# A stencil layer behind a mixture of experts: the gated expert outputs of pairs 1 to 3 are added onto x by accumulating DMAs of GpSimd's queue

## The chip, the cores and the metric

The kernel runs on one core of one Trainium2 chip. The metric is the device time of one execution in microseconds (us). The core has five engines with a queue of instructions each: TensorE (PE in the profile, its weight loads PEld), VectorE (DVE), ScalarE (ACT), GpSimd (POOL) and SyncE (SP, which here only issues DMAs). They run at the same time and are held in order by semaphores: an instruction raises one, another waits for its value.

## What is computed

Two layers stand one behind the other. The first (left unchanged here) normalises x, chooses two of eight experts for each token, runs the experts, and adds the two expert outputs, each times its gate, onto x. The second is a stencil layer on a field `f` of 8 images of 256 x 256:

```python
def _forward(x, ...):                      # layer 0, mixture of experts
    ...
    y = jnp.einsum('ned,ne->nd', eout, combine)   # two experts per token, weighted by their gates
    return x + y.reshape(x.shape)

def _L1_cond_ref(f, A_grid, B_grid, dt):   # layer 1, stencil
    Af = A_grid[None] * f[:, None]
    Bf = B_grid[None] * f[:, None]
    gradv_Af = _grad(Af[:, 0], 1) + _grad(Af[:, 1], 2)
    gradvv_Bf = _grad2(Bf[:, 0], 1) + _grad2(Bf[:, 1], 2) + _grad(_grad(Bf[:, 2], 2), 1) + ...
    df = -gradv_Af + gradvv_Bf * 0.5
    f_new = f + df * dt[:, None, None]
    return jnp.maximum(f_new, 0.0)
```

`_grad` and `_grad2` are first and second differences along an axis. The field that enters layer 1 is x + gate1 * y1 + gate2 * y2, where y1 and y2 are the rows that the two experts of a token gave.

## The kernel before, in words

A token is one row of 256 floats. x lies in SBUF for the whole kernel as `x_sb` (128 partitions x 16 tiles x 256); the rows of the experts go to a DRAM tensor `y_rows` (y1 first, then y2) by GpSimd's indirect DMAs (`scatter`, L716), 128 rows or 128 KB each.

The stencil stage starts when the last scatter has landed. It works on four **pairs** (g = 0 to 3) of images; a pair is a tile of 128 x 1024 floats (512 KB). Its buffers come twice, by the parity of g: `Y1`, `Y2` (the loaded expert rows; the profile calls both `t_y`), `F0` (x plus the first gated output) and `FV` (the field; the profile calls F0 and FV `t_f`), `FD` (the field times dt, `t_fd`), `GG` (`t_keep`), `GF` (`t_kept`), and products of them. What each engine does for a pair, in the order of its own queue:

- **SyncE**: loads Y1 and Y2 from `y_rows` (L429 in quarters for pair 0, L435 in 512 KB for the others, two pairs ahead at most), and later stores the result of each pair (L439, L444).
- **ScalarE**: `FD` = dt times the field, two halves (L654), when the field is there; then `keep(g+1)` (L630); then `gated(g+1)`: it multiplies the four tiles of Y1 and then the four of Y2 of the next pair by their gates, in place (L641), and raises `t_gated` after each of the two; then the output of the pair before (`relu_out`, L617; for the last pair L667).
- **VectorE**: `center(g)` = GG times the field (L1279); `products(g)`, eight long and four short instructions (L1285 to L1298); `add_up(g+1)`: F0 = Y1 + x (L1245) and FV = Y2 + F0 (L1248), each behind its `t_gated`; `along_columns(g)` (L1303). For pair 0 the gates are applied and the sums made by VectorE itself (L1255).
- **TensorE**: for each pair 20 matmuls of 128 x 512 plus 4 for the columns, all on L896: first `t_kept`, then `t_b0f`, then `t_u`, and the `t_cols` ones of a pair when `along_columns` is done.
- **GpSimd**: nothing after its last scatter.

The order in each queue is the order in which the program is written. `link(...)` makes VectorE wait for its own last instruction to have been written before it goes on (semaphore `chain`).

Of the kernel before, what the change touches and what calls it, by code (L numbers as in the profile page):

```python
# [7 lines left out]
ALU = mybir.AluOpType  # L8
# [8 lines left out]
NB, T, D = 8, 256, 256  # L17
# [103 lines left out]
def moe_then_stencil(nc, x, ids, dt, exp_w1, exp_b1, exp_w2, exp_b2, a_grid, b_grid, small, consts, out):  # L121
# [4 lines left out]
    with ctx:  # L126
# [3 lines left out]
        def sem(name):  # L130
            return ctx.enter_context(nc.semaphore(name))
# [5 lines left out]
        x_sb = sb("x_sb", [P, NJ, D])  # L137
        cst = sb("cst", [P, C_ALL])
        ident = cst[:, C_IDENT:C_IDENT + P]
        gates = sb("gates", [P, TOPK, NJ])  # L140
# [124 lines left out]
        with ExitStack() as phase:  # L265
            def own(name, shape, dt_=F32):
# [3 lines left out]
            Y1, Y2, F0, FV, FD, GG, GF, PA, PB, CC, U1, U2, PP, PQ, SM, OUT = (  # L270
                [own(f"{n}_{par}", [P, 4 * D])[:, :] for par in range(2)]
                for n in ("t_y1", "t_y2", "t_f0", "t_f", "t_fd", "t_keep", "t_kept", "t_a0f", "t_b2f", "t_d1b2f",
                          "t_u1", "t_b0f", "t_pf", "t_qf", "t_cols", "t_out"))
# [49 lines left out]
        y_first = [[sem(f"y{c}_first{i}") for i in range(2)] for c in range(TOPK)]  # L323
        t_first = sem("t_first")
        t_f, t_u2 = sem("t_f"), sem("t_u2")
        t_u1, t_s, t_gf, t_mm, t_relu = (sem(n) for n in ("t_u1", "t_s", "t_gf", "t_mm", "t_relu"))
        t_keep, t_fd, t_gated = sem("t_keep"), sem("t_fd"), sem("t_gated")
        out_dma = [sem(f"out_dma{i}") for i in range(3)]
        grids_ok = sem("grids_ok")
# [8 lines left out]
        block = ctx.enter_context(nc.Block())  # L338

        NPAIR = NB // 2  # L340
        TURNS = 6
        FIRST, ROUNDS = 4, 3
        assert NS == FIRST + TURNS * ROUNDS + 1
# [24 lines left out]
        def _(sp):  # L368
# [60 lines left out]
                    sp.dma_start(buf[0][:, 2 * D * i:2 * D * i + 2 * D].rearrange("p (j d) -> p j d", j=2),  # L429
                                 y_rows_tok[c, :, 2 * i:2 * i + 2, :]).then_inc(y_first[c][i], 16)  # L430
            for g in range(1, NPAIR):
                if g >= 2:
                    sp.wait_ge(t_f, g - 1)
                for c, buf in enumerate((Y1, Y2)):
                    sp.dma_start(buf[g % 2].rearrange("p (j d) -> p j d", j=4),  # L435
                                 y_rows_tok[c, :, 4 * g:4 * g + 4, :]).then_inc(y_in[c][g % 2], 16)
# [4 lines left out]
            g = NPAIR - 1  # L441
# [11 lines left out]
        def _(act):  # L453
# [191 lines left out]
            for g in range(NPAIR):  # L645
                if g >= 2:
                    act.wait_ge(t_s, g - 1)
                    act.wait_ge(t_u2, g - 1)
                for i in range(2):
                    if g == 0 and i == 0:  # L650
                        act.wait_ge(t_first, 1)
                    else:
                        act.wait_ge(t_f, g + 1)
                    last = act.activation(FD[g % 2][:, 512 * i:512 * i + 512], FV[g % 2][:, 512 * i:512 * i + 512],  # L654
                                          ACT.Copy, scale=dt_b[:, 2 * g + i:2 * g + i + 1])
                last.then_inc(t_fd, 1)
                if g < NPAIR - 1:
                    keep(g + 1)
                    gated(g + 1)
                if g >= 1:  # L660
                    relu_out(g - 1)
# [10 lines left out]
        @block.gpsimd  # L672
        def _(pool):
            pool.memset(half[:, :], -0.5).then_inc(half_set, 1)
            pool.wait_ge(half_set, 1)

            def number(out, pattern):

                pool.iota(out, pattern=pattern, base=0, channel_multiplier=0,
                          allow_small_or_imprecise_dtypes=True).then_inc(iota_ok, 1)  # L680


            for i in range(NB + 3):
                if i < NB:
                    pool.wait_ge(var1_ok, i + 1)
                    pool.tensor_tensor(rs1[:, 2 * i:2 * i + 2], var1[:, 2 * i:2 * i + 2], half[:, 0:2],
                                       ALU.pow).then_inc(rs1_ok, 1)
                if i >= 3:
                    pool.wait_ge(var2_ok, i - 2)
                    pool.tensor_tensor(rs2[:, i - 3, :], var2[:, i - 3, :], half[:, 0:KD],  # L690
                                       ALU.pow).then_inc(rs2_ok, 1)
            number(tile_of[:, :], [[P, TOPK * NJ]])
            number(col_of[:, :, :], [[1, NC], [0, TOPK * NJ]])
            number(row_of[:, :, :], [[1, P], [0, TOPK * NJ]])

            def gather(k, m):
                s, par = at_slot(k, m), k % 2
                pool.wait_ge(src_ok, s + 1)
                if k >= 2:
                    pool.wait_ge(tr_done, s - 1)  # L700
                pool.sem_inc(pool_go, 1)
                for t in range(width(k)):
                    pool.indirect_dma_start(  # L703
                        out=gathered[:, par, t, :], out_offset=None, in_=h_rows,
                        in_offset=bass.IndirectOffsetOnAxis(ap=src_cur[:, par, t:t + 1], axis=0),
                    ).then_inc(rows_in[par], 16)

            def scatter(k, m, halves=False):
                s, par = at_slot(k, m), k % 2
                pool.wait_ge(y_half if halves else y_ok, 1 if halves else s + 1)  # L710
                pool.wait_ge(dst_ok, s + 1)
                pool.sem_inc(pool_go, 1)
                for t in range(width(k)):
                    if halves and t == 1:
                        pool.wait_ge(y_ok, s + 1)
                    pool.indirect_dma_start(  # L716
                        out=y_rows, out_offset=bass.IndirectOffsetOnAxis(ap=dst_cur[:, par, t:t + 1], axis=0),
                        in_=y_sb[:, par, t, :], in_offset=None, bounds_check=TOPK * N - 1, oob_is_err=False,
                    ).then_inc(y_out[par], 16)

            pool.wait_ge(hrows_out, 16 * NJ)
            for k in range(FIRST):
                gather(k, None)
            for k in range(2, FIRST):
                gather(k + 2, None)
                scatter(k - 2, None)
            with pool.Fori(1, ROUNDS + 1) as m:
                for k in range(FIRST, FIRST + TURNS):
                    gather(k + 2, m)
                    scatter(k - 2, m)  # L730
            scatter(NS - 3, None)
            scatter(NS - 2, None)
            scatter(NS - 1, None, halves=True)


        @block.tensor
# [186 lines left out]
        def _(dve):  # L923
            steps = [0]

            def link(ins):

                steps[0] += 1
                ins.then_inc(chain, 1)
                dve.wait_ge(chain, steps[0])  # L930
# [99 lines left out]
            for c, src in enumerate((lg, lg2)):  # L1030
# [4 lines left out]
                                              op0=ALU.mult, op1=ALU.add))  # L1035
# [200 lines left out]
                ends = v.rearrange("p r (s c) -> p r s c", c=4)  # L1236
                return ends[:, :, 0:D // 4:D // 4 - 1, :]

            def add_up(g):
                if g >= 2:  # L1240
                    dve.wait_ge(t_fd, g - 1)
                if g > 0:

                    dve.wait_ge(t_gated, 2 * g - 1)
                    link(dve.tensor_tensor(F0[g % 2], Y1[g % 2],  # L1245
                                           x_sb[:, 4 * g:4 * g + 4, :].rearrange("p j d -> p (j d)"), ALU.add))
                    dve.wait_ge(t_gated, 2 * g)
                    last = dve.tensor_tensor(FV[g % 2], Y2[g % 2], F0[g % 2], ALU.add)  # L1248
                else:
                    for i in range(2):  # L1250
                        for c, y, dst in ((0, Y1, F0), (1, Y2, FV)):
                            dve.wait_ge(y_first[c][i], 16)
                            for j in range(2 * i, 2 * i + 2):
                                at = slice(D * j, D * j + D)
                                last = dve.scalar_tensor_tensor(  # L1255
                                    out=dst[0][:, at], in0=y[0][:, at], scalar=gates[:, c, j:j + 1],
                                    in1=x_sb[:, j, :] if c == 0 else F0[0][:, at], op0=ALU.mult, op1=ALU.add)
                            if c == 0:
                                link(last)
                        if i == 0:  # L1260
                            last.then_inc(t_first, 1)
                last.then_inc(t_f, 1)

            def wide(v):
# [7 lines left out]

            def center(g):
                par = g % 2
                dve.wait_ge(t_f, g + 1)
                dve.wait_ge(t_keep, g + 1)
                if g >= 2:
                    dve.wait_ge(t_mm, g - 1)
                dve.tensor_tensor(GF[par], GG[par], FV[par], ALU.mult).then_inc(t_gf, 1)  # L1279

            def products(g):
                par = g % 2
# [20 lines left out]
                dve.tensor_tensor(rows_of(SM[par])[:, :, 1:D - 1], pv[:, :, 2:D], qv[:, :, 0:D - 2],  # L1303
                                  ALU.add).then_inc(t_s, 1)

            add_up(0)
            for g in range(NPAIR):
                center(g)
                products(g)
                if g + 1 < NPAIR:  # L1310
                    add_up(g + 1)
                along_columns(g)


# [19 lines left out]
```

## Time and profile before

| | us |
|---|---|
| Time before, median of 3 runs | 395.35 (393.88 to 395.98) |
| The profiled execution: its own time | 395.92 |
| its span in the trace | 393.8 |
| VectorE busy | 284.7 (72% of the span) |
| ScalarE busy | 256.3 (65%) |
| TensorE matmuls busy | 330.6 (84%) |
| GpSimd busy | 130.0 (33%) |
| Stencil stage, from the first center to the end | 337.24 to 393.8 |

The profile's page has busy times of the engines, the span in 40 equal slices of 9.85 us (a digit is the busy share in tenths), DMA queues, the chain of work that ended last, and groups of instructions by line. The trace behind it can be asked for the instructions in order of time, for waits, for the chain piece by piece, for DMAs, and for the busy time within given stretches. A line number is that of the kernel before. The median of the runs and the profiled execution's time differ by 0.57 us; the span is 2.12 us shorter than the profiled execution's time.

### The profile page before, as it was taken

The numbers are of one execution on the slowest core, as the hardware profiler recorded it, in microseconds if no ns is written. First come the engines' busy times: TensorE is split into PE (matmuls) and PEld (weight loads), VectorE is DVE, ScalarE is ACT, GpSimd is POOL, SyncE is SP. The second block draws the span as 40 slices with busy tenths as digits, with TensorE's granted clock in tenths as the row PEclk, the third lists the DMA queues.
The fourth block names the chain that finished last, engine by engine and source line by source line (L and its number), as shares of the span: only waits on it lengthen the run. The fifth ranks groups of instructions, "written<-read, shape, count | busy, mean of one in ns | idle before, by whom it ended". The sixth has DMA issues, their size and how long they took to land.

```text
span 393.8 us, 7288 instructions
## 1 busy us (share of the span) xinstructions
PE 330.6 (84%) x2424; PEld 298.4 (76%) x2424; DVE 284.7 (72%) x500; ACT 256.3 (65%) x467; POOL 130.0 (33%) x103
## 2 busy tenths in 40 slices
PE   1676232889999999999999999999999991687976
PEld 1565232889999999999999999999999990233422
DVE  4696773657767768678777776866876852999994
ACT  2578032677696988779779779887976822543521
POOL 1245304233415545543551543554454031000000
PEclk9998655789999999999999999999999997599999
DMA  8903252973657776865775776677577004631111
GB/s 278 322 27 106 83 214 65 318 245 101 229 194 248 263 256 216 287 186 197 267 250 153 258 248 238 241 262 242 188 230 253 0 31 113 208 106 53 53 54 53
DMA packets 49204, 72.21 MB, mean 183 GB/s; under 512 B 3229, under 2 KB 40479, under 8 KB 49056
## 3 DMA queue, kind: packets, MB, share of 16 engines
q1 hardware_dynamic: 45056, 62.13, 47.1%
q0 software_dynamic: 3792, 9.45, 7.5%
q10 hardware_dynamic: 336, 0.39, 0.3%
q8 instruction: 10, 0.16, 0.2%
q14 instruction: 10, 0.08, 0.1%
HBM read 63.56 MB, written 9.31 MB: 185 GB/s over the span
## 4 chain that ended last, share of the span: by engine, by line
PE 70%; DVE 15%; DMA 5%; issue 4%; ACT 3%; POOL 2%; SPq 0%; POOLq 0%; DVEq 0%; ACTq 0%
PE psum L847 32%; PE psum L869 29%; PE psum L896 3%; PE psum L826 2%; DMA raw_b<-in_L_cond_exp_w_dram 2%; PE psum L813 1%; DMA t_y<-y_rows 1%; DVE st L965 1%; DMA x_sb<-in_x_dram 1%; POOL rs L690 1%; DVE t_f L1245 1%; DVE t_b0f L1290 1%; DVE t_pf L1297 1%; DVE t_cols L1303 1%; DVE t_kept L1279 1%
## 5 line engine op out<-in xcount | busy, mean ns | idle before, releaser
L847 PE MATMUL psum<-slot_h,w_split 128*128 128x256 f32 (+1 forms) x1104 | 136.4, 284 | 4.3 <-DVE slot_h L1147 4.3
L847 PEld LDWEIGHTS psum<-slot_h,w_split 128*128 128x128 f32 x1104 | 134.6, 196 | 4.9 <-issue 4.9
L869 PE MATMUL psum<-w_split,hid 128*128 128x256 f32 x936 | 117.8, 285 | 0.2 <-issue 0.2
L869 PEld LDWEIGHTS psum<-w_split,hid 128*128 128x128 f32 x936 | 113.7, 192 | 0.3 <-issue 0.3
L703 POOL DMA_INDIRECT gathered<-h_rows,src_cur x40 | 60.3, 1507 | 143.7 <-DVE src_cur L1130 109.3
L564 ACT ACTIVATE relu<-psum,b_cur 128x256 f32<-128x256 f32 (+1 forms) x184 | 70.0, 444 | 19.9 <-PE psum L847 15.1
L1141 DVE TENSOR_TENSOR w_split<-raw_b,w_split 128x2048 fp32r<-128x2048 f32 x23 | 52.7, 2292 | 22.1 <-ACT w_split L546 22.1
L1135 DVE TENSOR_TENSOR w_split<-raw_a,w_split 128x2048 fp32r<-128x2048 f32 x23 | 52.6, 2287 | 18.7 <-ACT w_split L539 11.4
L1154 DVE TENSOR_TENSOR hid<-relu,hid 128x512 fp32r<-128x512 f32 (+1 forms) x92 | 52.8, 605 | 17.6 <-ACT hid L573 16.2
L716 POOL DMA_INDIRECT y_rows<-y_sb,dst_cur x39 | 52.4, 1344 | 29.3 <-DVE y_sb L1173 13.2
L539 ACT ACTIVATE w_split<-raw_a 128x2048 fp32r<-128x2048 f32 x23 | 44.2, 1921 | 26.9 <-DMA raw_a<-in_L_cond_exp_w_dram 26.7
L573 ACT ACTIVATE hid<-relu 128x512 fp32r<-128x512 f32 (+1 forms) x92 | 50.5, 581 | 0.0
L546 ACT ACTIVATE w_split<-raw_b 128x2048 fp32r<-128x2048 f32 x23 | 44.4, 1932 | 4.0 <-DMA raw_b<-in_L_cond_exp_w_dram 4.0
L654 ACT ACTIVATE t_fd<-t_f,dt_b 128x512 f32<-128x512 f32 x8 | 5.5, 717 | 28.6 <-DVE t_f L1248 20.1
L1147 DVE TENSOR_TENSOR slot_h<-psum,slot_h 128x512 fp32r<-128x512 f32 (+1 forms) x23 | 14.0, 609 | 12.3 <-ACT slot_h L553 10.4
L896 PE MATMUL psum<-t_kept,cst 128*128 128x512 f32 x16 | 9.4, 719 | 12.5 <-DVE t_kept L1279 12.5
L826 PE MATMUL psum<-cst,gathered 128*128 128x128 f32 x80 | 13.3, 282 | 5.7 <-DMA gathered<-h_rows,src_cur 5.7
L778 PE MATMUL psum<-eye_rw,hT 128*128 128x136 f32 x64 | 12.6, 360 | 6.3 <-ACT hT L494 6.2
L778 PEld LDWEIGHTS psum<-eye_rw,hT 128*128 128x128 f32 x64 | 11.0, 254 | 8.1 <-ACT hT L494 6.2
L1173 DVE TENSOR_TENSOR y_sb<-psum,b_all 128x512 f32<-128x512 f32 (+1 forms) x23 | 13.6, 593 | 4.0 <-PE psum L869 4.0
L553 ACT ACTIVATE slot_h<-psum 128x512 fp32r<-128x512 f32 (+1 forms) x23 | 12.6, 546 | 6.0 <-PE psum L826 6.0
L896 PEld LDWEIGHTS psum<-t_kept,cst 128*128 128x128 f32 x16 | 3.5, 223 | 16.6 <-DVE t_kept L1279 12.7
(157 smaller groups left out, 282.8 us busy)
## 6 DMA issues: line engine op xcount, KB each, us to landing
raw_a<-in_L_cond_exp_w_dram SPq DMA_DIRECT2D x23, 1024.0 KB, 7.9
raw_b<-in_L_cond_exp_w_dram SPq DMA_DIRECT2D x23, 1024.0 KB
t_y<-y_rows SPq DMA_DIRECT2D x6, 512.0 KB, 4.9
x_sb<-in_x_dram SPq DMA_DIRECT2D x4, 512.0 KB, 7.1
h_rows<-h_tok SPq DMA_DIRECT2D x16, 128.0 KB, 2.2
out_dram<-t_out SPq DMA_DIRECT2D x3, 512.0 KB, 2.9
b_all<-in_L_cond_exp_b_dram SPq DMA_DIRECT2D x1, 1024.0 KB, 9.8
t_y<-y_rows SPq DMA_DIRECT2D x4, 256.0 KB, 3.7
```

Source lines behind the costliest of these rows:

```text
L539: act.activation(w_split[:, 0, par, 0, :], w1_raw[par], ACT.Copy).then_inc(w1_hi, 1)
L546: act.activation(w_split[:, 1, par, 0, :], w2_raw[par], ACT.Copy).then_inc(w2_hi, 1)
L564: last = act.activation(relu[:, bank, i, 0:n], banks[bank][:, ST * i:ST * i + n], ACT.Relu, bias=b1_cur[:, par, blk:blk + 1])
L573: act.activation(hid[:, par, 0, 2 * bank:2 * bank + 2, 0:n], relu[:, bank, :, 0:n], ACT.Copy).then_inc(hid_hi, 1)
L703: pool.indirect_dma_start(out=gathered[:, par, t, :], out_offset=None, in_=h_rows, in_offset=bass.IndirectOffsetOnAxis(ap=src_cur[:, par, ...
L716: pool.indirect_dma_start(out=y_rows, out_offset=bass.IndirectOffsetOnAxis(ap=dst_cur[:, par, t:t + 1], axis=0), in_=y_sb[:, par, t, :], i ...
L847: last = pe.matmul(banks[bank][:, ST * (blk % 2):ST * (blk % 2) + rows], w_split[:, 0, par, w, at:at + P], slot_h[:, par, h, k, 0:rows], s ...
L869: last = pe.matmul(banks[bank][:, D * t:D * t + D], hid[:, par, h, blk, P * t:P * t + P], w_split[:, 1, par, w, D * blk:D * blk + D], star ...
L896: return pe.matmul(banks[2 * g + q].rearrange("p (i d) -> p i d", i=2), w, v[:, k, :, :], start=start, stop=stop)
L1135: dve.tensor_tensor(w_split[:, 0, par, 1, :], w1_raw[par], w_split[:, 0, par, 0, :].bitcast(F32), ALU.subtract).then_inc(w1_lo, 1)
L1141: dve.tensor_tensor(w_split[:, 1, par, 1, :], w2_raw[par], w_split[:, 1, par, 0, :].bitcast(F32), ALU.subtract).then_inc(w2_lo, 1)
L1154: dve.tensor_tensor(hid[:, par, 1, 2 * bank:2 * bank + 2, 0:n], relu[:, bank, :, 0:n], hid[:, par, 0, 2 * bank:2 * bank + 2, 0:n].bitcast( ...
```

## The change

Pairs 1 to 3 no longer have `add_up`. When ScalarE has gated Y1 of a pair, GpSimd issues a DMA that reads Y1 from SBUF and adds it to the pair's 128 x 1024 floats of `x_sb`, in place; when that has landed and Y2 is gated too, a second DMA adds Y2. Its semaphore `y2_added` is what ScalarE's FD, VectorE's center and SyncE's load of pair 3 now wait for; the field of pairs 1 to 3 is read from `x_sb` (`field(g)`) and no longer from FV. Pair 0 is as it was.

```diff
+        def field(g):
+            return FV[0] if g == 0 else x_sb[:, 4 * g:4 * g + 4, :].rearrange("p j d -> p (j d)")
...
             for g in range(1, NPAIR):
-                if g >= 2:
-                    sp.wait_ge(t_f, g - 1)
+                if g == 2:
+                    sp.wait_ge(t_f, 1)
+                elif g > 2:
+                    sp.wait_ge(y2_added, 16 * (g - 2))
                 for c, buf in enumerate((Y1, Y2)):
...
                     if g == 0 and i == 0:
                         act.wait_ge(t_first, 1)
+                    elif g == 0:
+                        act.wait_ge(t_f, 1)
                     else:
-                        act.wait_ge(t_f, g + 1)
-                    last = act.activation(FD[g % 2][:, 512 * i:512 * i + 512], FV[g % 2][:, 512 * i:512 * i + 512],
+                        act.wait_ge(y2_added, 16 * g)
+                    last = act.activation(FD[g % 2][:, 512 * i:512 * i + 512], field(g)[:, 512 * i:512 * i + 512],
...
             scatter(NS - 1, None, halves=True)
+
+            for g in range(1, NPAIR):
+                pool.wait_ge(t_gated, 2 * g - 1)
+                pool.dma_start(field(g), Y1[g % 2], accum_op=ALU.add).then_inc(y1_added, 16)
+                pool.wait_ge(t_gated, 2 * g)
+                pool.wait_ge(y1_added, 16 * g)
+                pool.dma_start(field(g), Y2[g % 2], accum_op=ALU.add).then_inc(y2_added, 16)
...
-            def add_up(g):
-                if g >= 2:
-                    dve.wait_ge(t_fd, g - 1)
-                if g > 0:
-
-                    dve.wait_ge(t_gated, 2 * g - 1)
-                    link(dve.tensor_tensor(F0[g % 2], Y1[g % 2],
-                                           x_sb[:, 4 * g:4 * g + 4, :].rearrange("p j d -> p (j d)"), ALU.add))
-                    dve.wait_ge(t_gated, 2 * g)
-                    last = dve.tensor_tensor(FV[g % 2], Y2[g % 2], F0[g % 2], ALU.add)
-                else:
...
             def center(g):
                 par = g % 2
-                dve.wait_ge(t_f, g + 1)
+                if g == 0:
+                    dve.wait_ge(t_f, 1)
+                else:
+                    dve.wait_ge(y2_added, 16 * g)
                 dve.wait_ge(t_keep, g + 1)
                 if g >= 2:
                     dve.wait_ge(t_mm, g - 1)
-                dve.tensor_tensor(GF[par], GG[par], FV[par], ALU.mult).then_inc(t_gf, 1)
+                dve.tensor_tensor(GF[par], GG[par], field(g), ALU.mult).then_inc(t_gf, 1)
...
-            add_up(0)
+            add_up()
             for g in range(NPAIR):
                 center(g)
                 products(g)
-                if g + 1 < NPAIR:
-                    add_up(g + 1)
                 along_columns(g)
```

VectorE's queue from the last products of pair 0 to the first of pair 1, before (the names in brackets are the semaphores that an instruction waits for):

```order
L1298 TENSOR_TENSOR t_qf<-gr,t_fd 128x1024
L1245 TENSOR_TENSOR t_f_1<-t_y_1,x_sb 128x1024 [waits t_gated,chain]
L1248 TENSOR_TENSOR t_f<-t_y_1,t_f_1 128x1024 [waits t_gated,chain]
L1303 TENSOR_TENSOR t_cols<-t_pf,t_qf 128x4x254
L1279 TENSOR_TENSOR t_kept<-t_keep,t_f 128x1024 [waits t_keep,t_f]
L1285 TENSOR_TENSOR t_b2f<-gr,t_fd 128x1024 [waits t_fd]
```

The same place now:

```order
L1306 TENSOR_TENSOR t_pf<-gr,t_fd 128x1024
L1307 TENSOR_TENSOR t_qf<-gr,t_fd 128x1024
L1312 TENSOR_TENSOR t_cols<-t_pf,t_qf 128x4x254 [waits chain]
L1288 TENSOR_TENSOR t_kept<-t_keep,x_sb 128x1024 [waits t_keep,y2_added]
L1294 TENSOR_TENSOR t_b2f<-gr,t_fd 128x1024 [waits t_fd]
```

The two additions are gone from between the products and the columns, the columns now wait for the products directly, and center waits for the semaphore of the second accumulating DMA.

GpSimd's queue at its end, now (in the kernel before it ended with the last scatter into y_rows):

```order
L725 DMA y_rows<-y_sb,dst_cur 4096x256 [waits y_ok]
L746 DMA x_sb<-t_y_1 128x1024 [waits t_gated]
L749 DMA x_sb<-t_y_1 128x1024 [waits y1_added,t_gated]
L746 DMA x_sb<-t_y_0 128x1024 [waits t_gated]
L749 DMA x_sb<-t_y_0 128x1024 [waits y1_added,t_gated]
```

Two DMAs for each pair were added, the second of each behind the landing of the first; pair 3 has the same two rows again.

ScalarE's queue from the gating of pair 1 to that of pair 2, now (before, the row of L663 read t_f and waited for t_f, at L654, with the same rows around it):

```order
L648 ACTIVATE t_y_1<-t_y_1,gates 128x256 [waits y1_in1]
L648 ACTIVATE t_y_1<-t_y_1,gates 128x256 x3
L663 ACTIVATE t_fd<-x_sb,dt_b 128x512 [waits y2_added] x2
L637 ACTIVATE t_keep<-grid,ones,dt_n 128x512 [waits t_gf]
L637 ACTIVATE t_keep<-grid,ones,dt_n 128x512
L648 ACTIVATE t_y_0<-t_y_0,gates 128x256 [waits y0_in0]
```

Nothing moved in ScalarE's queue; the gating of the next pair stands behind the instruction that waits for the second accumulating DMA of this pair.

## Rows read from the trace of the kernel before

**Rows 1.** Busy time by stretch: busy us (instructions) of each engine, granted clock, DMA.

```profile
core 0: us, PE busy (x) PEld busy (x) DVE busy (x) ACT busy (x) POOL busy (x), PEclk, DMA share, GB/s
325.00:337.24 12.24, 1.00 (x9) 0.79 (x7) 3.95 (x9) 2.24 (x3) 1.54 (x2) 0.68 0.52 157
337.24:350.60 13.36, 11.12 (x20) 4.60 (x20) 13.22 (x15) 6.33 (x13) 0.00 (x0) 0.78 0.28 93
350.60:363.96 13.36, 11.10 (x24) 4.31 (x24) 13.22 (x16) 6.77 (x14) 0.00 (x0) 1.00 0.36 118
363.96:377.32 13.36, 11.10 (x24) 4.31 (x24) 13.22 (x17) 6.85 (x14) 0.00 (x0) 1.00 0.11 39
```

**Rows 2.** The chain of work that ended last, around pair 1's additions and the end.

```profile
345.91 1.15 DVE t_qf L1298
...
347.08 1.24 DVE t_f L1245
348.31 0.02 issue
348.33 0.04 DVE t_f L1248
348.37 1.11 issue
349.48 1.21 DVE t_cols L1303
...
384.90 5.52 PE psum L896 x12
```

**Rows 3.** Timeline, VectorE and ScalarE from pair 1's gating: start, us, engine, line.

```profile
339.28 3.29 ACT L641 ACTIVATE t_y<-t_y,gates 128x256 f32<-128x256 f32 x8
...
348.33 1.23 DVE L1248 TENSOR_TENSOR t_f<-t_y,t_f 128x1024 f32<-128x1024 f32 x1
...
349.60 1.33 ACT L654 ACTIVATE t_fd<-t_f,dt_b 128x512 f32<-128x512 f32 x2 [7.02 <-DVE t_f L1248]
...
352.25 3.29 ACT L641 ACTIVATE t_y<-t_y,gates 128x256 f32<-128x256 f32 x8
...
356.47 24.43 SPq L439 DMA_DIRECT2D out_dram<-t_out  x3
```

**Rows 4.** Timeline, the start of pair 3 on ScalarE and VectorE.

```profile
376.39 1.34 ACT L654 ACTIVATE t_fd<-t_f,dt_b 128x512 f32<-128x512 f32 x2 [6.51 <-DVE t_f L1248]
377.32 1.22 DVE L1279 TENSOR_TENSOR t_kept<-t_keep,t_f 128x1024 f32<-128x1024 f32 x1
...
378.45 1.22 DVE L1285 TENSOR_TENSOR t_b2f<-gr,t_fd 128x1024 f32<-128x1024 f32 x1
```

**Rows 5.** The instructions on the gated rows of pairs 1 to 3, min/median/max ns.

```profile
L641 ACT ACTIVATE t_y<-t_y,gates x24: 491/493/496, 339.3 to 368.5; 128x256 f32<-128x256 f32 x24
```

**Rows 6.** Timeline, the last scatter and the first load behind it.

```profile
326.03 0.42 DVE L1173 TENSOR_TENSOR y_sb<-psum,b_all 128x256 f32<-128x256 f32 x1 [2.34 <-PE psum L869]
...
327.23 0.98 POOL L716 DMA_INDIRECT y_rows<-y_sb,dst_cur  x1 [1.68 <-DVE y_sb L1173]
329.36 1.91 SPq L429 DMA_DIRECT2D t_y<-y_rows  x4
```

**Rows 7.** DMA issues by line: count, KB each, median us to landing.

```profile
t_y<-y_rows SPq DMA_DIRECT2D x6, 512.0 KB, 4.9
...
out_dram<-t_out SPq DMA_DIRECT2D x3, 512.0 KB, 2.9
...
out_dram<-t_out SPq DMA_DIRECT2D x2, 256.0 KB, 2.2
```

**Rows 8.** Timelines of VectorE and of GpSimd at two long indirect DMAs.

```profile
289.93 2.29 DVE L1135 TENSOR_TENSOR w_split<-raw_a,w_split 128x2048 fp32r<-128x2048 f32 x1 [1.01 <-ACT w_split L539]
...
301.04 2.29 DVE L1135 TENSOR_TENSOR w_split<-raw_a,w_split 128x2048 fp32r<-128x2048 f32 x1 [1.17 <-ACT w_split L539]
...
290.36 2.69 POOL L703 DMA_INDIRECT gathered<-h_rows,src_cur  x1 [0.31 <-issue]
...
302.22 1.98 POOL L716 DMA_INDIRECT y_rows<-y_sb,dst_cur  x1 [0.30 <-issue]
```

**Rows 9.** Timeline, TensorE's first matmuls of the stencil stage.

```profile
338.52 3.78 PE L896 MATMUL psum<-t_kept,cst 128*128 128x512 f32 x4 [12.53 <-DVE t_kept L1279]
...
377.45 1.98 PE L896 MATMUL psum<-t_cols,cst 128*128 128x512 f32 x4 [2.21 <-DVE t_cols L1303]
```

More of the change, by code:

```diff
@@ L326, in moe_then_stencil @@
         t_u1, t_s, t_gf, t_mm, t_relu = (sem(n) for n in ("t_u1", "t_s", "t_gf", "t_mm", "t_relu"))
+        y1_added, y2_added = sem("y1_added"), sem("y2_added")
         t_keep, t_fd, t_gated = sem("t_keep"), sem("t_fd"), sem("t_gated")
@@ L1237, in edge_cols, with add_up @@
                 return ends[:, :, 0:D // 4:D // 4 - 1, :]
-            def add_up(g):
-                if g >= 2:
-                    dve.wait_ge(t_fd, g - 1)
-                if g > 0:
-                    dve.wait_ge(t_gated, 2 * g - 1)
-                    link(dve.tensor_tensor(F0[g % 2], Y1[g % 2],
-                                           x_sb[:, 4 * g:4 * g + 4, :].rearrange("p j d -> p (j d)"), ALU.add))
-                    dve.wait_ge(t_gated, 2 * g)
-                    last = dve.tensor_tensor(FV[g % 2], Y2[g % 2], F0[g % 2], ALU.add)
-                else:
[L1250 to L1261, printed above, removed]
+            def add_up():
+                for i in range(2):
+                    for c, y, dst in ((0, Y1, F0), (1, Y2, FV)):
+                        dve.wait_ge(y_first[c][i], 16)
+                        for j in range(2 * i, 2 * i + 2):
+                            at = slice(D * j, D * j + D)
+                            last = dve.scalar_tensor_tensor(
+                                out=dst[0][:, at], in0=y[0][:, at], scalar=gates[:, c, j:j + 1],
+                                in1=x_sb[:, j, :] if c == 0 else F0[0][:, at], op0=ALU.mult, op1=ALU.add)
+                        if c == 0:
+                            link(last)
+                    if i == 0:
+                        last.then_inc(t_first, 1)
                 last.then_inc(t_f, 1)
```

## The prediction

> **What bounds the kernel now.** I read the busy time by stretch first, then the chain of work that ended last, then the instructions in order of time. From 337.24 us to the end the kernel is in the stencil stage. The stretches of [rows 1] are one pair each: VectorE is busy 13.22 of every 13.36 us, ScalarE 6.3 to 6.9, TensorE 11.1, GpSimd not at all. The chain of [rows 2] runs through VectorE alone (the "issue" pieces of about 1.1 us are time in which the next VectorE instruction was already running or being written) until the columns of pair 2, and from there through TensorE, twelve matmuls in 5.52 us at the end. So an instruction taken off VectorE in pairs 0 to 2 is worth its time, as long as nothing else comes last. The reader is to see in [rows 3] what stands behind that: ScalarE waits 7.02 us for pair 1's field, because it had gated the pair's rows long before VectorE came to add them (gated from 339.28 on, added at 347.08).
>
> **What is removed.** Two additions for each of three pairs. From the first of them to the columns: 349.48 - 347.08 = 2.40 us [rows 2]. The columns follow the products directly, and their wait for the products costs what the wait between t_qf and L1245 cost, 0.02 to 0.03, which is inside this difference. VectorE's own work per pair falls from 13.36 to 10.96 us, over three pairs by 7.2 us. That is the floor: no gain beyond it.
>
> **What is added, and where it lies.** The sum of a pair now takes two DMAs one behind the other. Call L the time from the release of one of them (the end of the gating, or the landing of the first) to the landing seen by whoever waits. The work between two pairs becomes a loop that VectorE is not in:
>
> - Pair 1: Y1 is gated at 339.28 + 3 x 0.40 + 0.49 = 340.97 (eight activations in 3.29 us, each 0.49 long, so 0.40 apart) [rows 3, 5]. Y2's gating takes another 1.60 us and lies beside the first DMA. So the field of pair 1 is there at 340.97 + 2L.
> - From a field to the next pair's gated Y1 ScalarE does FD, keep and four gatings: before from 349.56 (end of L1248) to 352.25 + 1.69 = 353.94, so 4.38 us [rows 3]. All of this order stays, and is now behind the landing.
> - Field of pair 2: 340.97 + 2L + 4.38 + 2L. Field of pair 3: 340.97 + 8.76 + 6L = 349.73 + 6L.
> - From the last field on, the end is as before: FD takes 1.34 us after a start 0.04 behind the field, and t_b2f needs it, at the field + 1.41. Before, t_b2f of pair 3 started at 378.45 [rows 4]. The end moves by 349.73 + 6L + 1.41 - 378.45 = **6L - 27.3 us**, as long as this is above -7.2.
>
> So six DMAs in a row decide, and the change breaks even at L = 4.55 us. VectorE stays the bound only if 4.38 + 2L is under 10.96, so for L under 3.3.
>
> **What L is.** The trace has no accumulating DMA, and no plain one of GpSimd. The nearest row is GpSimd's last scatter [rows 6]: VectorE's write ends at 326.45, GpSimd starts at 327.23 and is busy for 0.98 us, and the load of SyncE that waited for the landing starts at 329.36. From release to release that is 2.91 us for 128 KB. Four times the bytes: the stores of 512 and 256 KB land in 2.9 and 2.2 us [rows 7], so 0.7 us for each 256 KB, and 384 KB more are 1.05 us. A copy would be 3.96 us. An accumulation has to read the old values of x too; I take these as another 512 KB at the same rate, 1.4 us. **L = 5.4 us.** The lower end: GpSimd starts at once (0.78 less) and the second read is hidden (1.4 less), 3.2; the store of SyncE in 2.9 is nearly the same. The upper end: the loads of 512 KB that shared the engines landed in 4.9, which is 2.0 over the store [rows 7]; added to 5.4, and with 1.2 for a wait on VectorE (below), 8.6. I take the value near the scatter's row, since it is the only one of GpSimd's own queue to start in the same way.
>
> Beside it, the store of the pair before: ScalarE's output of it follows the gatings, and the store was issued at 356.47, 6.9 us after the field [rows 3], when the first accumulation of the next pair (from 4.4 to 9.8 us after the field) moves its bytes. Its 512 KB cost up to 1.4 us there, in pairs 2 and 3; half of it each is 1.4 in all. The loads of pair 3 start at the field of pair 1 and land within 4.9, before the accumulation moves bytes: nothing. Center on VectorE reads `x_sb` in place of FV, the same size: nothing. Behind the wait of ScalarE's FD stand keep, the gatings and the output of the pair before; all but the output are in the 4.38, and the output's store has a pair's time. SyncE's stores stand behind its load of pair 3, which waits for pair 1's field, well before the first store is due. GpSimd has nothing behind its DMAs.
>
> The sum: 6 x 5.4 - 27.3 + 1.4 = **+6.5 us**. Against the profiled execution, 395.92, that is 402.4; its median runs are 0.57 lower, 395.35, so I say **401.9 us** for a median.
>
> **The first rule weighed.** What a DMA of GpSimd pays here is 2.91 us for 128 KB, the wake-up included [rows 6]. The Trainium skill, DMA: Bandwidth & Descriptors, section "Anatomy of one DMA", gives about 2.0 us plus the bytes at 436 GB/s; by it, as an estimate, 512 KB would be 3.2 us and the change would give the whole 7.2 us, as in the quick rival below.
>
> **The rivals.**
> 1. *The DMAs are quick, and the change is faster.* The place is the release of the field; the price is L near the lower end: 3.2 gives the floor, 395.35 - 7.2 = 388.2; 4.0 gives -3.3, 392.0. It decides below L = 4.55. For it: SyncE's 512 KB in 2.9, and a 0.78 us wake-up that may belong to indirect DMAs. Against: every accumulation has two reads to do. 0.17.
> 2. *About even*, L from 4.2 to 4.9, within 2 us of 395.35: 0.12.
> 3. *GpSimd is held up by VectorE's additions and products.* Two long indirect DMAs in [rows 8] show the mechanism: the gather that starts at 290.36, inside a VectorE instruction with two SBUF inputs (289.93 to 292.22), ends 0.83 after that instruction; the scatter of 302.22, inside one that ends at 303.33, ends 0.87 after it. Both are otherwise about 1 us. In the stencil stage VectorE runs such instructions of 1.22 us back to back, while all six DMAs are issued. A mean wait of half of one is 0.6, six times 3.7: 395.35 + 6.5 + 3.7 = 405.6; a full one each time would be +7.3, 409. For it: the rows. Against: an indirect DMA reads its list of rows from SBUF, and the new ones have none. 0.15. The Trainium skill, SBUF — State Buffer, section "Who interferes with whom", says that a VectorE instruction with two SBUF inputs blocks a GpSimd one that reads SBUF, and not one that only writes; by that, these DMAs would pay only if issuing them reads SBUF, which no run here shows yet.
> 4. *The addition inside the DMA runs well below the copy's rate.* Nothing in the trace speaks for or against it. At half the rate, 2.8 us more each, six times 16.8: about 418.7. TensorE would then be idle so long between pairs that its clock may fall, as after its 12.5 us of idling before 338.52, where four matmuls took 3.78 in place of 1.98 us [rows 9]; that could add up to 2 us at the end. 0.16.
> 5. *My forecast*, L from 4.9 to 6.6 with little waiting: +2 to +12 us, 397.4 to 407.5: 0.40.
>
> **How the numbers follow.** Faster and slower are counted from 0.5% on, 2 us, about what a measurement of this kernel can tell from no change. Faster 0.17 (rival 1), same 0.12 (rival 2), slower 0.71 (3, 4 and 5). The range reaches into rival 1 to L of about 4.3, 394, and into rival 4 to 415, which leaves some 0.1 out at either side.
>
> **What the profile after would show.** GpSimd: six DMAs from 341 on in pairs, the second of each starting when the first has landed. VectorE: the columns of pair 0 at 347.1, then idle until the field at 340.97 + 10.8 = about 352, and some 4 to 5 us idle before each of the next two centers, with the semaphore of GpSimd's DMA as releaser. ScalarE's FD starts together with VectorE's center. The distance from one center to the next is 15 to 16 us, where it was 13.36. It would be wrong if VectorE is busy without gaps at 10.96 per pair (rival 1), if GpSimd's issue itself is over 1.2 us long and ends with a VectorE instruction (rival 3), or if its issue is short but the landing takes 7 us and more (rival 4). If FD started earlier or the store stood before the gatings, the 4.38 would be wrong; if the two DMAs overlapped, the factor 6.

## The result: 0.9% slower, less than forecast

| | before | changed |
|---|---|---|
| median us (range, runs) | 394.94 (393.88 to 395.98, 6) | 399.21 (397.61 to 400.56, 6) |
| ratio, 95% interval | | 1.0088 (1.0065 to 1.0111) |
| profiled execution, its span | 395.92, 393.8 | 397.61, 395.8 |
| VectorE busy us | 284.7 | 278.5 |

The sign was forecast, the size was not: +6.5 us against +3.5 (2.6 to 4.4) by the ratio; the two medians lie 4.3 us apart. Two later sets of runs of the same kernel gave 1.0087 and 1.0069. The profiled execution happened to be the quickest of the six.

The busy time by stretch in the changed kernel; the stretches begin at each pair's center, as in [rows 1]:

```profile
core 0: us, PE busy (x) PEld busy (x) DVE busy (x) ACT busy (x) POOL busy (x), PEclk, DMA share, GB/s
...
336.51:350.33 13.82, 12.54 (x24) 5.35 (x24) 10.95 (x14) 5.33 (x12) 1.84 (x2) 0.79 0.65 160
350.33:364.65 14.32, 11.47 (x25) 4.24 (x24) 11.04 (x14) 6.85 (x13) 1.71 (x2) 1.00 0.73 183
364.65:379.00 14.35, 12.26 (x24) 5.02 (x24) 11.04 (x13) 6.85 (x13) 1.72 (x2) 0.88 0.49 110
```

VectorE's work per pair fell from 13.22 to 11.0 us, as forecast, and the pairs became longer: 13.82, 14.32 and 14.35 where they were 13.36. VectorE now idles about 3 us in each. The chain of work that ended last shows what took its place, here from pair 1's gating to pair 2's field (start, us, what):

```profile
338.64 1.61 ACT t_y L648 x4
340.25 0.30 issue
340.55 4.64 DMA x_sb<-t_y
345.19 0.03 issue
345.22 0.02 POOLq L748
345.23 0.51 issue
345.75 4.55 DMA x_sb<-t_y
350.30 0.02 issue
350.33 1.33 ACT t_fd L663 x2
351.66 1.41 ACT t_keep L637 x2
353.07 1.61 ACT t_y L648 x4
354.68 0.28 issue
354.96 4.62 DMA x_sb<-t_y
359.58 0.02 issue
359.60 0.02 POOLq L748
359.62 0.49 issue
360.11 4.52 DMA x_sb<-t_y
364.63 0.02 issue
```

VectorE is not in it (compare [rows 2]). From gating to field it is 350.30 - 340.25 = 10.05 us, then 354.68 - 350.30 = 4.38 of ScalarE, then 9.95 again. Before pair 3 ScalarE has 4.45, and the two DMAs 9.90. One DMA, release to release, is therefore **5.0 us**, the mean of six.

For the comparison of kernels below I use one distance that earlier stages can't shift: from the first center to t_b2f of pair 3. Before it is 378.45 - 337.24 = 41.21 us [rows 1, 4], changed 380.45 - 336.51 = 43.94, so **+2.7 us**:

```profile
336.51 1.22 DVE L1288 TENSOR_TENSOR t_kept<-t_keep,t_f 128x1024 f32<-128x1024 f32 x1
...
379.00 1.23 DVE L1288 TENSOR_TENSOR t_kept<-t_keep,x_sb 128x1024 f32<-128x1024 f32 x1 [2.99 <-DMA x_sb<-t_y]
380.45 1.23 DVE L1294 TENSOR_TENSOR t_b2f<-gr,t_fd 128x1024 f32<-128x1024 f32 x1 [0.22 <-ACT t_fd L663]
```

### The profile page after: what moved, and what is told of

Read it like the earlier page. It is cut to its first block, busy times and chain, and to the rows that moved or that the text cites. A ratio compares the mean times of both kernels' runs of the same rounds, so it can differ in the third digit from the quotient of the medians.

```text
span 395.8 us, 7285 instructions
## 1 busy us (share of the span) xinstructions
PE 331.4 (84%) x2424; PEld 298.7 (75%) x2424; DVE 278.5 (70%) x494; ACT 255.8 (65%) x467; POOL 137.1 (35%) x109
## 4 chain that ended last, share of the span: by engine, by line
PE 69%; DMA 12%; ACT 7%; DVE 7%; issue 3%; POOL 1%; SPq 0%; POOLq 0%; ACTq 0%; DVEq 0%
PE psum L863 32%; PE psum L885 28%; DMA x_sb<-t_y 7%; PE psum L912 2%; PE psum L842 2%; DMA raw_b<-in_L_cond_exp_w_dram 1%; PE psum L829 1%; DMA t_y<-y_rows 1%; ACT t_y L648 1%; PE psum L794 1%; ACT t_keep L637 1%; ACT t_fd L663 1%; DMA x_sb<-in_x_dram 1%; ACT relu L571 1%; POOL rs L695 1%
## 5 line engine op out<-in xcount | busy, mean ns | idle before, releaser
L725 POOL DMA_INDIRECT y_rows<-y_sb,dst_cur x39 | 53.8, 1379 | 29.3 <-DVE y_sb L1189 13.2
L912 PE MATMUL psum<-t_kept,cst 128*128 128x512 f32 x16 | 11.3, 843 | 17.9 <-DVE t_kept L1288 17.9
L663 ACT ACTIVATE t_fd<-x_sb,dt_b 128x512 f32<-128x512 f32 x6 | 4.0, 714 | 23.6 <-DMA x_sb<-t_y 23.6
L912 PE MATMUL psum<-t_b0f,cst 128*128 128x512 f32 x32 | 15.3, 623 | 1.8 <-DVE t_b0f L1299 1.8
```

The lines of the kernel that those rows point to most:

```text
L725: pool.indirect_dma_start(out=y_rows, out_offset=bass.IndirectOffsetOnAxis(ap=dst_cur[:, par, t:t + 1], axis=0), in_=y_sb[:, par, t, :], i ...
L912: return pe.matmul(banks[2 * g + q].rearrange("p (i d) -> p i d", i=2), w, v[:, k, :, :], start=start, stop=stop)
```

## The experiments

All distances are from the profiled executions; all ratios are to the kernel before, run beside on the same chip. "Six copies" and "one DMA a pair" leave out a part of the computation, so they show what a DMA costs and are no candidates.

| kernel | distance us (to 41.21) | ratio, interval |
|---|---|---|
| changed, second set | 43.92 (+2.7) | 1.0087 (1.0057 to 1.0117) |
| changed, third set | 43.90 (+2.7) | 1.0069 (1.0043 to 1.0095) |
| six copies, no adding (computes less) | 34.43 (-6.8) | 0.9831 (0.9791 to 0.9871) |
| one DMA a pair (computes less) | 34.13 (-7.1) | 0.9808 (0.9771 to 0.9845) |
| gated early | 37.16 (-4.1) | 0.9909 (0.9879 to 0.9938) |
| mixed | 35.17 (-6.0) | 0.9848 (0.9831 to 0.9865) |
| pair 1 on VectorE | 36.43 (-4.8) | 0.9902 (0.9880 to 0.9924) |
| halves | 42.94 (+1.7) | 1.0066 (1.0043 to 1.0089) |
| before, gated early | 41.23 (0.0) | 1.0002 (0.9985 to 1.0018) |
| changed, idle time filled | 44.19 (+3.0) | 1.0112 (1.0079 to 1.0145) |

### The changed kernel again

No edit.

> The changed kernel, unaltered, timed again beside the kernel before, because in its profiled execution the stencil stage explains only +2.7 us of the +4.3 us between the medians. Theory A (the loop of two DMAs in series and ScalarE's 4.36 us is the whole of it): ratio 1.007, +2 to +3.5 us, and the six DMAs again 5.0 us each. Theory B (something else as well, as the TensorE clock, which fell to 0.88 between pairs 2 and 3 in the first profile, or slower DMAs in most executions): ratio 1.009 to 1.012, and a profile whose stencil stage is longer than 59.3 us with DMAs of over 5.2 us or a clock under 0.9 in the last pair.

Measured 398.70 against 395.88. The DMAs and the distance are the same to 0.1 us, so the loop is stable, and TensorE's granted clock in the last pair is 1.00: of theory B's signs the profile has none. The ratio, 1.0087, is 3.4 us, inside theory A's +2 to +3.5 though above its 1.007. What the 0.7 us over the trace are comes at the end of this section.

### Copies in place of additions

```diff
-                pool.dma_start(field(g), Y1[g % 2], accum_op=ALU.add).then_inc(y1_added, 16)
+                pool.dma_start(field(g), Y1[g % 2]).then_inc(y1_added, 16)
```

and the same for Y2.

> The six DMAs copy instead of adding (the same bytes, the same queue, no reading of the old values); the field of pairs 1 to 3 is then the gated y2 alone, so part of the computation is left out. Theory A1 (the addition is paid as a second read of 512 KB): the bytes take 1.3 us instead of 2.6, each DMA 3.7 us from release to release instead of 5.0, and the kernel ends 7 to 8 us earlier than the changed one, at about 391. Theory A2 (adding costs next to nothing, the 5.0 us are what any DMA of 512 KB of GpSimd takes): L stays 4.8 to 5.0 and the time stays within 1.5 us of the changed kernel.

GpSimd's timeline:

```profile
341.70 0.60 POOL L746 DMA_DIRECT2D x_sb<-t_y  x1 [12.90 <-ACT t_y L648]
345.16 0.57 POOL L749 DMA_DIRECT2D x_sb<-t_y  x1 [2.86 <-DMA x_sb<-t_y]
352.75 0.54 POOL L746 DMA_DIRECT2D x_sb<-t_y  x1 [7.02 <-ACT t_y L648]
```

and its DMA issues, beside the same row of the changed kernel (KB each, us to landing):

```profile
x_sb<-t_y POOLq DMA_DIRECT2D x6, 512.0 KB, 2.9
```

```profile
x_sb<-t_y POOLq DMA_DIRECT2D x6, 512.0 KB, 4.6
```

Pair 1's gating ends at 341.40 (four of the eight activations from 339.71 on) and FD starts at 348.11: 3.36 us for each DMA, 3.5 in pair 2. So adding costs 1.5 to 1.6 us of the 5.0 (1.7 from issue to landing): about 0.3 in GpSimd's own issue (0.85 to 0.95 in place of 0.54 to 0.60) and the rest in the transfer. The row of GpSimd's DMA queue shows the transfer itself (packets, MB, and the packets' time as a share of the 16 DMA engines' time from 338 to 390 us), first with copies, then with additions:

```profile
q0 software_dynamic: 864, 3.15, 14.7%
```

```profile
q0 software_dynamic: 864, 3.15, 32.1%
```

The packets and the bytes are the same, and their time is 2.2 times as long: of 52 us, for each of six DMAs, 2.8 us of each DMA engine in place of 1.3. The Trainium skill, DMA: Bandwidth & Descriptors, section "Anatomy of one DMA", has about 2.0 us plus the bytes at 436 GB/s, an estimate of 3.2 us for 512 KB; the copy is near it (2.9 from issue to landing), the accumulation, 4.6, is 1.4 over. The Trainium skill, Collectives: The Full Stack, section "The bandwidth ceiling: the fold count and why AG ≠ RS ≠ AR", puts the lower rate of a reduce-scatter ring between cores down to the two source reads of its additions; the 2.2 times of this case fit that, though the runs here show no reads by themselves. Theory A1 held, with 3.4 us for a DMA where it had 3.7. The time was 389.78, 8.9 us under the changed kernel where 7 to 8 were expected, and VectorE's 10.96 per pair became the bound again (-6.8 of a possible 7.2).

### One DMA for each pair

```diff
-                pool.wait_ge(t_gated, 2 * g - 1)
-                pool.dma_start(field(g), Y1[g % 2], accum_op=ALU.add).then_inc(y1_added, 16)
                 pool.wait_ge(t_gated, 2 * g)
-                pool.wait_ge(y1_added, 16 * g)
-                pool.dma_start(field(g), Y2[g % 2], accum_op=ALU.add).then_inc(y2_added, 16)
+                pool.dma_start(field(g), Y1[g % 2], accum_op=ALU.add).then_inc(y2_added, 16)
```

> Only y1 is added (one DMA for each pair instead of two, issued when both are gated); y2 is left out of the field of pairs 1 to 3. Theory A: the loop is 4.36 + 1.6 + 5.0 = 10.96 us, as long as VectorE's own 10.96, so VectorE is busy almost without gaps and the kernel is 6.5 to 7.5 us faster than before (388). Theory B (the loss is not the series of two DMAs but that center and FD start together behind a DMA, or the clock): over 391.

387.92, distance -7.1 of a possible 7.2 (the ratio says 7.6 us, with an interval from 6.1 to 9.1). VectorE had no wait for a DMA left, as the centers of pairs 1 and 2 show:

```profile
347.29 1.22 DVE L1285 TENSOR_TENSOR t_kept<-t_keep,x_sb 128x1024 f32<-128x1024 f32 x1
...
358.25 1.22 DVE L1285 TENSOR_TENSOR t_kept<-t_keep,x_sb 128x1024 f32<-128x1024 f32 x1
```

One accumulating DMA a pair, under VectorE's work, costs next to nothing here; two in series behind ScalarE's 4.4 us do.

### Gated early

```diff
                 if g < NPAIR - 1:
                     keep(g + 1)
-                    gated(g + 1)
-                if g >= 1:
+                if g == 0:
+                    gated(1)
+                    gated(2)
+                else:
                     relu_out(g - 1)
+                if g == 1:
+                    gated(3)
```

> All six accumulating DMAs as in the changed kernel; ScalarE alone is written in another order: it gates pair 2 right after pair 1, and pair 3 after keep(2) and the first output, so its 4.36 us no longer stand between one pair's field and the next one's DMAs. Theory A: pair 1 still waits for its field until 350.3 (2.8 us), pairs 2 and 3 are bound by VectorE (10.96) or by two DMAs (10.0 to 10.2); the kernel is 6 us faster than the changed one and 3 to 4 us faster than before. Rival (the DMAs in a row slow each other or GpSimd, or the two DMAs in series alone are too long): gain over the changed kernel under 3 us.

392.02 against 395.88, and 6.7 us under the changed kernel timed beside it (398.70). The same six DMAs, now as follows:

```profile
340.62 0.95 POOL L750 DMA_DIRECT2D x_sb<-t_y  x1 [12.73 <-ACT t_y L648]
345.82 0.89 POOL L753 DMA_DIRECT2D x_sb<-t_y  x1 [4.24 <-DMA x_sb<-t_y]
346.41 1.18 POOL L750 DMA_DIRECT2D x_sb<-t_y  x1
354.02 0.86 POOL L753 DMA_DIRECT2D x_sb<-t_y  x1 [6.44 <-DMA x_sb<-t_y]
```

Pair 2's y1 is issued right behind pair 1's y2. The DMAs are not quicker for it: the median from issue to landing is 5.1 us where it was 4.6, and the one of 354.02, which has loads and a store beside it, takes 6.4. VectorE's centers:

```profile
350.45 1.23 DVE L1292 TENSOR_TENSOR t_kept<-t_keep,x_sb 128x1024 f32<-128x1024 f32 x1 [2.81 <-DMA x_sb<-t_y]
...
361.65 1.22 DVE L1292 TENSOR_TENSOR t_kept<-t_keep,x_sb 128x1024 f32<-128x1024 f32 x1
...
372.61 1.22 DVE L1292 TENSOR_TENSOR t_kept<-t_keep,x_sb 128x1024 f32<-128x1024 f32 x1
```

Pair 1 still waits 2.81 us for its DMAs, the other two wait for nothing. With the same six DMAs, slower ones at that, the order of one engine's queue made the difference between loss and gain.

### Control: the kernel before, gated early

The same edit of ScalarE's order in the kernel before.

> Control: the kernel before, with ScalarE's order of the early gating alone and no accumulating DMA. In the kernel before ScalarE waited 6.5 to 7.0 us for each field with the rows long gated, so theory A expects no change, ratio 0.998 to 1.002. If the early gating gains by itself, part of what it gave the changed kernel was not the loop.

Ratio 1.0002. So the new order is worth 6.7 us only where it breaks the loop, and nothing by itself.

### Mixed, and pair 1 wholly on VectorE

Mixed: gated early, and pair 1's y2 added by VectorE. The core of the edit:

```diff
-            for g in range(1, NPAIR):
+            pool.wait_ge(t_gated, 1)
+            pool.dma_start(x_sb[:, 4:8, :].rearrange("p j d -> p (j d)"), Y1[1],
+                           accum_op=ALU.add).then_inc(y1_added, 16)
+            for g in range(2, NPAIR):
...
                 center(g)
                 products(g)
+                if g == 0:
+                    dve.wait_ge(t_gated, 2)
+                    dve.wait_ge(y1_added, 16)
+                    dve.tensor_tensor(FV[1], Y2[1], x_sb[:, 4:8, :].rearrange("p j d -> p (j d)"),
+                                      ALU.add).then_inc(t_f, 1)
                 along_columns(g)
```

> The early gating, and pair 1's field made differently: y1 by an accumulating DMA, y2 by one addition on VectorE (1.22 us), pairs 2 and 3 wholly by DMAs. Theory A (what matters is only whether a field is there when VectorE comes to it): no wait of VectorE for a DMA is left, 2.40 us saved in two pairs and 1.2 in one, 6.0 us faster than before, ratio 0.985, and 2 us faster than the early gating alone. Rival (six DMAs or the clock take something back elsewhere): no better than the early gating alone, ratio 0.99.

The other kernel has, in place of that addition and of GpSimd's first DMA:

```diff
+                if g == 0:
+                    dve.wait_ge(t_gated, 1)
+                    link(dve.tensor_tensor(F0[1], Y1[1], x_sb[:, 4:8, :].rearrange("p j d -> p (j d)"), ALU.add))
+                    dve.wait_ge(t_gated, 2)
+                    dve.tensor_tensor(FV[1], Y2[1], F0[1], ALU.add).then_inc(t_f, 1)
```

> As the mixed kernel, but pair 1 has both additions on VectorE as before, and four DMAs are left. Theory A: 2.40 us saved in two pairs, 4.8 us faster than before, ratio 0.988, 1.2 us slower than the mixed kernel. Rival: the same as the mixed kernel or as the early gating alone.

Mixed: 389.35 against 395.35, the quickest of the kernels that compute everything. Its distance of -6.0 is the expected sum of 2 x 2.40 and 1.2. With both additions of pair 1 on VectorE it is -4.8 in the trace, as expected, and 391.14 in time; the ratio, 0.9902, is 3.9 us and its interval (3.0 to 4.7) stops just short of the 4.8, which stays open. The addition of pair 1 in the mixed kernel starts right behind the products, with no wait; the DMA of y1 had landed before 346.30, when GpSimd issued the next one:

```profile
346.90 1.22 DVE L1328 TENSOR_TENSOR t_f<-t_y,x_sb 128x1024 f32<-128x1024 f32 x1
348.04 1.21 DVE L1318 TENSOR_TENSOR t_cols<-t_pf,t_qf 128x1016 f32<-128x1016 f32 x1
```

### Halves

```diff
+                for at, done in zip(half_of, (y1_added, y1_late)):
+                    pool.dma_start(field(g)[:, at], Y1[g % 2][:, at], accum_op=ALU.add).then_inc(done, 16)
...
+                for at, done in zip(half_of, (y1_added, y1_late)):
+                    pool.wait_ge(done, 16 * g)
+                    pool.dma_start(field(g)[:, at], Y2[g % 2][:, at], accum_op=ALU.add).then_inc(y2_added, 16)
```

> The changed kernel with each accumulating DMA cut into two of 256 KB (columns 0 to 511 and 512 to 1023), twelve in all, the halves of y2 each behind the same half of y1; ScalarE's order as in the changed kernel. If most of the 5.0 us of a DMA is a fixed part (wake-up, issue, first byte, landing), two half chains overlap and the pair's two sums take about 9.2 us instead of 10.0, the kernel 2.5 us faster than the changed one. If the bytes set the time, or GpSimd's issues of 0.9 us each add up, no gain or a loss of up to 1 us a pair.

A partial miss. The time was 398.26. Pair 1's sum took 349.54 - 340.43 = 9.1 us, as expected of overlapping half chains; pairs 2 and 3 took 10.0 (353.89 to 363.83, 368.25 to 378.19), no gain. The last half took 3.56 us from issue to landing in pair 1 and 4.21 and 4.17 in the others. Those two have the store of the pair before beside them and pair 1 has not, which may be why; it wasn't tried without the store. The distance fell by 1.0 and not by 2.5.

### Filling TensorE's idle time

In the first profile of the changed kernel TensorE's clock fell at the start of pair 2 (granted clock 0.88 in that pair's stretch; its t_kept matmuls took 3.51 us). It cost nothing there, since TensorE then still waited 2.09 us for pair 3's center. In the profile of the third set it fell at the start of the last pair, whose stretch has 0.88:

```profile
376.35 1.97 PE L912 MATMUL psum<-t_cols,cst 128*128 128x512 f32 x4
380.54 2.52 PE L912 MATMUL psum<-t_kept,cst 128*128 128x512 f32 x4 [2.22 <-DVE t_kept L1288]
383.45 4.58 PE L912 MATMUL psum<-t_b0f,cst 128*128 128x512 f32 x8 [0.39 <-DVE t_b0f L1299]
```

```profile
365.00:379.50 14.50, 11.19 (x24) 4.23 (x24) 11.19 (x14) 7.00 (x14) 1.72 (x2) 1.00 0.49 108
379.50:396.00 16.50, 12.26 (x24) 4.75 (x24) 10.79 (x13) 3.27 (x5) 0.00 (x0) 0.88 0.18 64
```

Eight t_b0f matmuls took 4.58 us where they take 3.70 in the last pair of the first profile, and from t_b2f to the last output it is 393.22 - 380.70 = 12.52 us in place of 392.45 - 380.45 = 12.00: 0.5 us.

```diff
                             last.then_inc(t_mm, 1)
+                    if g < NPAIR:
+                        for _ in range(5):
+                            pe.matmul(banks[7], ident, cst[:, C_D1:C_D1 + 512], start=True, stop=True)
```

> The changed kernel with five matmuls of 128 x 512 more behind the column matmuls of pairs 0, 1 and 2, into the last PSUM bank, whose content is not used before pair 3 starts it anew: TensorE's idle time of 2.2 us there is filled (2.1 us of work at the high clock). If executions in which the clock falls just before the last pair make up the 0.7 us between the trace (+2.7) and the medians (+3.4): no granted clock under 1.00 behind 350 us, ratio to before 1.006 to 1.007, and a narrower spread than the 4 us of the changed kernel. If the rest comes from elsewhere: ratio 1.0085 to 1.009 as before, or more, where the added matmuls delay the others.

> The changed kernel a third time, on the same chip as the run with filled idle time, to compare the two: ratio 1.0085 to 1.009.

```profile
380.91 4.46 PE L930 MATMUL psum<-cst 128*128 128x512 f32 x10
385.20 1.88 PE L912 MATMUL psum<-t_kept,cst 128*128 128x512 f32 x4
386.92 3.60 PE L912 MATMUL psum<-t_b0f,cst 128*128 128x512 f32 x8
```

The filling was sized wrongly: five matmuls are ten in the trace and took 4.46 us, not 2.1. The clock stayed at 1.00 behind 350.50 us. The spread did not become narrower (398.49 to 402.29), t_kept of the last pair started at 385.20, 4.5 us behind center's start at 380.72, and the kernel lost more than the clock could give back (1.0112). So the experiment doesn't settle how much of the medians the clock makes; what is shown is that a fall in the last pair occurs and costs 0.5 us in the execution that was profiled. The third set of the changed kernel, 1.0069, lies under the 1.0085 to 1.009 expected of it. The mean of the three ratios of the changed kernel is 1.0081, 3.2 us, against 2.7 in the trace; the 0.5 between them is inside each of the three intervals, and stays open.

## Why the prediction was right in kind and wrong in size

**What bounds the kernel, and what is removed.** Right. VectorE was the chain up to the columns of pair 2; where nothing else came late (one DMA a pair) a pair took 10.96 us in place of 13.36, 2.40 less as forecast, and the kernel gained 7.1 of the 7.2 us forecast as the floor.

**The loop.** Right: 349.73 + 6L, with ScalarE's 4.38 us between a field and the next DMA (measured 4.38 and 4.45). With the measured L the formula gives 6 x 5.0 - 27.3 = +2.7, what the trace shows. VectorE waited about 3 us for each field, where 4 to 5 were forecast, and the centers lay 13.8 to 14.4 us apart and not 15 to 16, both because L was too long. The steps that only asserted cover held too: SyncE's load of pair 3, keep, the read of `x_sb` by center.

**The value of L: the step that failed, as a size.** The forecast made the six DMAs and the store cost 6 x 5.4 + 1.4 = 33.8 us; they cost 29.9 (10.05 + 9.95 + 9.90), 3.9 less. Two terms were too high, the wake-up by 2.1 and the store by 1.4 us; with the rounding of 5.36 up to 5.4 (0.2) that is 3.7 of the 3.9. The terms one by one:
- *The wake-up*, 0.78 us each from the last scatter [rows 6]: measured 0.30 behind the gating and 0.56 from one DMA's landing to the issue of the next, 0.43 in the mean. Too high by 0.35 each, 2.1 us in all. The row of an indirect DMA was used for a plain one. Whether the indirect form makes the difference, or what else stands before the DMA in the queue, isn't shown. The prediction had named the doubt about the indirect form, and kept the term in full.
- *The store beside*, 1.4 us: measured nothing in this kernel. The accumulation with the store beside took 4.62 us from issue to landing, the one of pair 1 without it 4.64; it was the store that took longer, 3.8 us in place of 2.9 [rows 7]. That is not so everywhere: in the kernel with one DMA a pair, where the store is issued 0.6 us behind the accumulation and not 2.2, the two accumulations beside a store took 4.9 and 4.8 us and the one without 4.6, and those stores 5.4.
- *The second read*, 1.4 us each: measured 1.7 from issue to landing. The copy under it was 3.4 and not 3.96, which is the wake-up again and 0.2 less. The 0.3 too little for the read and the 0.2 to 0.3 too much for the copy cancel: from issue to landing the forecast had 5.36 - 0.78 = 4.58 us, and the six took 4.52 to 4.64. That this part came out so exactly is luck.

**The break-even.** At L = 4.55 it lay 0.45 us under the measured L, and each 0.1 us of L is 0.6 us of the kernel. The forecast is six times one unmeasured duration, so the sign hung on that 0.45 us, and the range, 394 to 415, holds the median.

**The rivals.** *Quick DMAs*: true of a copy (3.4 us, the kernel 6.7 us faster), not of an accumulation. *Held up by VectorE* [rows 8]: not so for the six plain DMAs. The second DMA of pair 1 is issued inside a VectorE instruction that reads two SBUF tensors:

```profile
345.09 1.22 DVE L1307 TENSOR_TENSOR t_qf<-gr,t_fd 128x1024 f32<-128x1024 f32 x1
...
345.75 0.89 POOL L749 DMA_DIRECT2D x_sb<-t_y  x1 [4.25 <-DMA x_sb<-t_y]
```

It ends at 346.64, only 0.33 after that instruction (346.31), where the indirect ones needed 0.83 and 0.87 from there on; no issue of the six was over 0.95 us. (Gated early, one is 1.18, issued right behind another accumulation; why wasn't looked into.) That agrees with the Trainium skill, SBUF — State Buffer, section "Who interferes with whom": an instruction with two SBUF inputs stops a GpSimd one that reads SBUF, and not one that only writes. *Adding below the copy's rate*: the transfer does take longer than a copy, but by 1.7 us, near the 1.4 that a second read was priced at, and not by 4.2.

**The chances.** Slower had 0.71, and the outcome lies at the lower edge of the forecast's own case, +2 to +12.

## What to carry to other kernels

Work handed from a busy engine to a DMA is free only if the result is there when it is needed: count the DMAs in series, then look at what else stands in that loop. Here 4.4 us of another engine's queue stood in it; moving that ahead turned +3 us into -4, and leaving one addition of the first pair, which has no time to prepare, on VectorE made it -6. Price a DMA from release to release, and by a row of the same kind: here the wake-up was 0.78 us in the row that the price came from, an indirect DMA, and 0.30 and 0.56 in the plain ones.

## What the runs showed of the hardware

- A 512 KB accumulating DMA of GpSimd from SBUF to SBUF lands in 4.5 to 4.6 us from issue, a copy in 2.9 (one of six in 3.2); the issue itself is 0.85 to 0.95 us against 0.54 to 0.60. Its packets keep the 16 DMA engines busy 2.2 times as long as those of the copy.
- A store of 512 KB issued 2.2 us behind it didn't slow it, and took 3.8 us in place of 2.9. Issued 0.6 us behind it, the store took 5.4 and the accumulation 4.8 to 4.9. With loads and a store beside it an accumulation took 6.4 us (gated early) and, with pair 1 on VectorE, 8.3.
- TensorE's clock fell from 2.4 GHz to 1.2 GHz for part of a pair after an idle time of 2.2 to 2.3 us that followed a stretch busy 11.2 to 11.9 of 14.3 us, once behind 350 us in each of the changed kernel's three profiles. After idle times of 1.8 to 2.25 us it stayed at 2.4 GHz in other pairs of the same profiles (before pair 3 in the first, before pair 2 in the third), and in the kernel before, with 2.21 us [rows 9] between stretches busy 11.1 of 13.36 us, at 1.00 from 350.60 us on [rows 1]. What decides it isn't shown.
